# Graph attention on one core: the softmax numerator placed in the one-hot, the relation factor applied by GpSimd, the sums in two banks

## The reference

```python
z = h @ W.T                                   # 6250 x 128
s_src = z @ w1;  s_dst = z @ w2
e = leaky_relu(s_src[src] + s_dst[dst], negative_slope=0.01)
rel_alpha = rel_emb[etype, 0]                 # 40 relations
m = segment_max(e, dst)
num = exp(e - m[dst])
den = segment_sum(num, dst)
alpha = num / den[dst]
h_agg = segment_sum((rel_alpha * alpha)[:, None] * z[src], dst)
return h_agg + bias_w
```

## Time and profile before

| | us |
|---|---|
| median of 3 executions | 10841.97 (10825.0 to 10871.25) |
| profiled execution, its time | 10860.68 |
| profiled execution, its span | 10859.2 |
| attention stage, first to last `look_all` | 3316.4 to 5276.4 |

### The profile page before, as it was taken

The page is one execution under the profiler, slowest core; times in us unless marked ns, Lnnn a source line. Parts: engine busy times, 40 slices in busy tenths (PEclk is TensorE's granted clock), DMA queues, the critical chain, the costliest instruction groups (busy, mean ns, idle before and its releaser), DMA issues. The chain is left out here.

```text
span 10859.2 us, 155042 instructions
## 1 busy us (share of the span) xinstructions
PE 8132.9 (75%) x38400; PEld 4994.6 (46%) x38401; DVE 4174.1 (38%) x9924; ACT 3269.5 (30%) x5403; POOL 5556.4 (51%) x5296
## 2 busy tenths in 40 slices
PE   2988888888875666655688897986887777777776
PEld 1544444444444555555433333333344555555554
DVE  5877777644335666665400000000002222222223
ACT  3012345655555665555200000000002222222222
POOL 5887887777720000000254556555435656566664
PEclk7999999999995666666788898997897777777777
DMA  3234455666644333222466676775672222222222
GB/s 111 75 112 142 150 186 199 222 209 207 214 172 143 121 114 106 98 91 90 175 238 263 241 287 231 290 282 195 262 270 85 62 58 61 59 62 62 62 60 55
DMA packets 563155, 1661.18 MB, mean 153 GB/s; under 512 B 115313, under 2 KB 312029, under 8 KB 519494
## 3 DMA queue, kind: packets, MB, share of 16 engines
q1 hardware_dynamic: 324442, 1129.76, 28.1%
q0 software_dynamic: 206976, 473.99, 14.9%
q10 hardware_dynamic: 31536, 54.94, 1.4%
HBM read 1174.46 MB, written 483.82 MB: 153 GB/s over the span
## 5 line engine op out<-in xcount | busy, mean ns | idle before, releaser
L920 PE MATMUL wide<-ring 128*128 128x392 bf16 x14112 | 2524.8, 340 | 551.8 <-DVE ring L850 269.1
L527 POOL DMA_INDIRECT z_got<-z_table,z_idx x1568 | 2102.0, 1341 | 595.2 <-issue 467.3
L1701 POOL DMA_INDIRECT l_rows<-h_table,l_recs x1568 | 1581.2, 1008 | 1169.9 <-DMA l_recs<-sorted_recs 720.7
L920 PEld LDWEIGHTS wide<-ring 128*128 128x128 bf16 x14112 | 1413.1, 100 | 1663.3 <-issue 907.3
L1610 POOL DMA_INDIRECT sorted_recs<-dn_rec_in,type_f x1568 | 1527.0, 974 | 1251.3 <-DMA dn_rec_in<-in_records 787.1
L1415 PE MATMUL wide<-stream,X 128*128 128x512 f32 (+1 forms) x2548 | 1148.9, 604 | 221.3 <-issue 201.9
L1055 POOL DMA_DIRECT2D rows<-z_edges x196 | 103.5, 528 | 2071.1 <-PE wide L362 1848.4
L373 PE MATMUL wide<-rows,onehot 128*128 128x130 f32 x3904 | 874.9, 413 | 286.2 <-DVE A L390 286.2
L373 PE MATMUL wide<-l_rows,l_onehot 128*128 128x128 f32 x3904 | 657.9, 321 | 503.4 <-issue 299.4
L373 PEld LDWEIGHTS wide<-rows,onehot 128*128 128x128 f32 x3904 | 810.5, 316 | 344.5 <-DVE A L390 344.5
L1415 PEld LDWEIGHTS wide<-stream,X 128*128 128x128 f32 x2548 | 497.5, 203 | 846.1 <-issue 827.5
(11 more groups left out here) (262 smaller groups left out, 8630.4 us busy)
## 6 DMA issues: line engine op xcount, KB each, us to landing
stream<-w_dense SPq DMA_DIRECT2D x252, 1792.0 KB
stream<-c_dense SPq DMA_DIRECT2D x84, 1792.0 KB
z_edges<-z_got POOLq DMA_DIRECT2D x196, 528.0 KB
rows<-z_edges POOLq DMA_DIRECT2D x196, 528.0 KB
dst_bc<-in_dst_row SPq DMA_DIRECT2D x196, 512.0 KB
c_dense<-A SPq DMA_DIRECT2D x49, 1568.0 KB
w_dense<-A SPq DMA_DIRECT2D x49, 1568.0 KB
c_dense<-H SPq DMA_DIRECT2D x49, 1568.0 KB
```

Of the source, the lines that this page charges most:

```text
L527: e.indirect_dma_start(out=z_got[:, s, t, :], out_offset=None, in_=z_table, in_offset=bass.IndirectOffsetOnAxis(ap=z_idx[:, s, t:t + 1], a ...
L920: ins = e.matmul(banks[:, bass.ds(to[v], 1), int(m > 0), 0:WC].rearrange("p a x -> p (a x)"), lhsT=slots[:, k, m * P:(m + 1) * P], rhs=slo ...
L1701: e.indirect_dma_start(out=rows[:, k, t, :], out_offset=None, in_=h_table, in_offset=bass.IndirectOffsetOnAxis(ap=recs[:, k, t, R_DST:R_DS ...
```

## The change

What it does, part by part:

- The one-hot of a tile is now made by `tensor_scalar` with two per-partition scalars: (iota == dst) * num. Eight instructions of 128 elements a pair take the place of two of 512. `num` is not copied into `rows` any more; the column of ones there gives the denominator.
- ACT's eight row scalings are gone. POOL multiplies the rows by the relation factor `rel`, in one `tensor_tensor` of 8 x 128 elements a group, after the DMA has landed.
- The degree is counted by ACT: the mask instruction accumulates into `seen`, a small one adds it to `deg_n`. `add_sums` has one instruction instead of two, and matmuls are 129 instead of 130 columns wide.
- The sums alternate between two banks (`pair_sums`). `half_ready[0]` no longer waits for the addition. The spread source scores alternate too (`s_rowed`), as do the mask (`mask_t`) and `q`. `away` and `mask_t` lie in `H`, which is free in this stage. Addresses that alternate come from a register (`parity`), with a register instruction each.
- ACT makes the masks of group g+1 while DVE is at group g. DVE does the sums of g-1 between the looks of g and `look_all` of g. TensorE turns the scores of g+1 before its looks of g.
- POOL loads three groups at the start; the load of g+3 follows the sums of g-1, and the product for g+1 stands behind it in POOL's queue.
- `s_max` is dropped: `u_node` keeps the running maximum.

```diff
 @block.gpsimd
+                for s in range(SLOTS - 1):
+                    load_rows(slice(s, s + 1), s)
                 with e.Fori(0, TURNS) as i:
                     for s in range(SLOTS):
-                        e.wait_ge(s_free[s], i + 1)
+                        e.wait_ge(s_rows[s], (i + 1) * 16)
                         e.sem_inc(note["pool"], 1)
-                        e.dma_start(rows[:, s, :, :], z_edges[bass.ds(i * SLOTS + s, 1), :, :, :].rearrange(
-                            "a p t w -> (a p) t w")).then_inc(s_rows[s], 16)
+                        e.tensor_tensor(rows[:, s, :, 0:F], rows[:, s, :, 0:F],
+                                        rel[:, bass.ds((i * SLOTS + s) * TILES, TILES)].unsqueeze(2).to_broadcast(
+                                            [P, TILES, F]), ALU.mult).then_inc(s_scaled, 1)
+                        if s == 0:
+                            e.wait_ge(s_free[SLOTS - 1], i + 1)
+                            load_rows(bass.ds(i * SLOTS + (SLOTS - 1), 1), SLOTS - 1)
+                        else:
+                            with e.If(i < TURNS - 1):
+                                e.wait_ge(s_free[s - 1], i + 2)
...
 @block.scalar
-                def scale_rows(g, s):
-                    e.wait_ge(s_w_, g + 1)
-                    for t in range(TILES):
-                        ins = e.activation(rows[:, s, t, 0:F], rows[:, s, t, 0:F], ACT.Copy,
-                                           scale=row_scale[:, t:t + 1])
-                    ins.then_inc(s_scaled, 1)
+                def masks(s, turn):
...
+                    with e.Fori(lo, hi) as b:
+                        at = parity(e, side, c)
+                        e.wait_ge(s_away_free, c)
+                        e.wait_ge(s_look, c)
+                        e.activation(away, dst_bc[:, k, :], ACT.Square, scale=FAR,
+                                     bias=far_node[:, bass.ds(b, 1)]).then_inc(s_away, 1)
+                        e.wait_ge(s_away, c)
+                        e.activation(flat(mask_t[:, bass.ds(at, 1), :]), away, ACT.Relu,
+                                     scale=-1.0, bias=one_f[:, 0:1], accum_out=seen[:, bass.ds(at, 1)]).then_inc(s_ot, 1)
+                        e.wait_ge(s_ot, c)
+                        e.activation(deg_n[:, bass.ds(b, 1)], seen[:, bass.ds(at, 1)], ACT.Identity,
+                                     bias=deg_n[:, bass.ds(b, 1)])
...
+                def ahead(g, s, turn):
+                    pick(s, turn)
+                    bring(g)
+                    masks(s, turn)
...
 @block.tensor
+                        turn_s(g + 1)
+                        looks(g, *ranges[s])
+                        spread_s(g + 1, (s + 1) % 2)
...
                 def sums(g, s, lo, hi):
                     e.wait_ge(s_scaled, g + 1)
-                    pe_sums(e, lo, hi, half_ready, half_done, rows[:, s, :, :], SW_, c2)
-                    mark(e, s_free[s])
+                    with e.Fori(lo, hi):
+                        e.reg_add(c2, c2, 1)
+                        at = parity(e, side, c2)
+                        for h in range(2):
+                            e.wait_ge(half_ready[h], c2)
+                            for t in range(4 * h, 4 * h + 4):
+                                ins = e.matmul(flat(pair_sums[:, bass.ds(at, 1), 0:MW]), lhsT=onehot[:, t, :],
+                                               rhs=rows[:, s, t, 0:MW], start=(t == 0), stop=(t == TILES - 1))
+                            ins.then_inc(half_done[h], 1)
...
 @block.vector
+                def sums(g, s, lo, hi):
+                    e.wait_ge(s_num, g + 1)
+                    with e.Fori(lo, hi) as b:
+                        for h in range(2):
+                            e.wait_ge(half_done[h], c2)
+                            if h:
+                                add_pair(...)
+                            for t in range(4 * h, 4 * h + 4):
+                                ins = e.tensor_scalar(onehot[:, t, :], iota[:, bass.ds(b * P, P)],
+                                                      dst_f[:, bass.ds(g * TILES + t, 1)], num[:, t:t + 1],
+                                                      ALU.is_equal, ALU.mult)
+                            ins.then_inc(half_ready[h], 1)
...
+                        sums(g - 1, s - 1, *ranges[s - 1])
                         e.wait_ge(s_looked, g + 1)
                         e.tensor_reduce(look_all ...)
...
                         e.tensor_tensor(e_edge[:, :], e_edge[:, :], look_all[:, :, 1], ALU.subtract).then_inc(s_ee, 1)
-                        sums(g - 1, s - 1, *ranges[s - 1])
-                        e.wait_ge(s_num, g + 1)
-                        e.tensor_copy(rows[:, s, :, F], num[:, :])
-                        e.tensor_tensor(row_scale[:, :], num[:, :], rel[:, bass.ds(g * TILES, TILES)], ALU.mult
-                                        ).then_inc(s_w_, 1)
```

More of the change, by code:

```diff
@@ L25 @@
 ZW = F + 4
[L26 removed]
+S_DST, S_SRC, S_PARTS = F, F + 1, 2 * (F + 2)
 PARTS = 4
@@ L381, in half_onehot, with add_sums @@
                                    ids.to_broadcast([P, 4, P]), ALU.is_equal)
[L383 removed]
+        def add_sums(e, b, width):
             to, new = A[:, bass.ds(b * width, width)], sums_bank[:, 0:width]
[L386 to L390 removed]
             return e.tensor_tensor(to, to, new, ALU.add)
@@ L424, in dve_sums_end @@
             e.sem_inc(note["dve"], 1)
-            add_sums(e, before, width, None if scales is None else scales.before())
+            add_sums(e, before, width)
             e.drain()
@@ L1065, in _, with pick @@
             def _(e):
-                def bring(g, i, s):
-                    e.wait_ge(s_rows[s], (i + 1) * 16)
+                c = counter(e, "l0_act_pairs", 1)
+                side = e.alloc_register("l0_act_side")
+                regs = [range_registers(e, f"l0_act{s}") for s in range(SLOTS)]
+                after = e.alloc_register("l0_act_after")
+                def pick(s, turn):
+                    e.wait_ge(s_rows[s], (turn + 1) * 16)
                     e.sem_inc(note["act"], 1)
@@ L1084, in _ @@
-                c = counter(e, "l0_act_pairs", 1)
-                regs = [range_registers(e, f"l0_act{s}") for s in range(SLOTS)]
+                    e.copy(s_src_t[:, :], turned).then_inc(s_brought, 1)
+                def ahead(g, s, turn):
+                    pick(s, turn)
+                    bring(g)
+                    masks(s, turn)
                 load_range(e, table_dst, 0, regs[0])
-                before, after = e.alloc_register("l0_act_before"), e.alloc_register("l0_act_after")
+                load_range(e, table_dst, 1, regs[1])
@@ L1088, in _ @@
                 for k in range(2):
                     e.sem_inc(s_bcf[k], 1)
-                e.reg_mov(before, 0)
-                for first in (s_away, s_ot, s_q, s_look, s_away_free, s_away_free):
-                    e.sem_inc(first, 1)
-                bring(0, 0, 0)
+                e.sem_inc(s_away, 1)
+                e.sem_inc(s_ot, 1)
+                e.sem_inc(s_sbc, 1)
+                e.sem_inc(s_away_free, 2)
+                e.sem_inc(s_look, 3)
+                e.copy(deg_n[:, :], zero_f[:, 0:1].to_broadcast([P, NB]))
@@ L1095, in _ @@
+                e.drain()
+                ahead(0, 0, 0)
                 with e.Fori(0, TURNS) as i:
@@ L1153, in spread_s, with looks @@
                     for t in range(TILES):
-                        ins = e.matmul(wide[:, t * P:(t + 1) * P],
+                        ins = e.matmul(s_rowed[k][:, t * P:(t + 1) * P],
                                        lhsT=spread[:, t * P:(t + 1) * P], rhs=s_src_t[:, :], start=True, stop=True)
                     ins.then_inc(s_sbc, 1)
+                def looks(g, lo, hi):
+                    e.wait_ge(s_ee, g + 1)
+                    e.sem_inc(note["pe"], 1)
+                    e.matmul(look, lhsT=zero_h[0:1, :], rhs=zero_h[0:1, 0:6 * TILES], start=True, stop=False)
+                    with e.Fori(lo, hi):
+                        e.reg_add(c, c, 1)
+                        at = parity(e, side, c)
+                        e.wait_ge(s_ot, c)
+                        e.wait_ge(s_q, c)
+                        e.sem_inc(note["pe"], 1)
+                        for t in range(TILES):
+                            ins = e.matmul(look[:, 6 * t:6 * t + 6],
+                                           lhsT=flat(mask_t[:, bass.ds(at, 1), t * P:(t + 1) * P]),
+                                           rhs=flat(q[:, bass.ds(at, 1), :]), start=False, stop=False)
+                        ins.then_inc(s_look, 1)
+                    e.matmul(look[:, 0:1], lhsT=zero_h[0:1, :], rhs=zero_h[0:1, 0:1], start=False, stop=True
+                             ).then_inc(s_looked, 1)
                 def sums(g, s, lo, hi):
@@ L1259, in _ @@
                             e.tensor_copy(m_node[:, bass.ds(b, 1)], m_now[:, 0:1])
-                            e.reg_add(c_last, c_last, 1)
```

(6 more changed lines are left out.)

236 lines of the change are left out of this document (119 added, 117 removed).

## The result

The changed kernel takes 11,280 us (median of 4 runs, 11,259.6 to 11,314.5) against 10,857 for the kernel before on the same chip: ratio 1.038, 95% interval 1.035 to 1.041. The profiled execution took 11,314 us (span 11,313).

The account below looks back on a forecast made before the run. No engine was full; VectorE's chain was taken to set the attention stage's pace. 10,861 - 77 (VectorE's own sum) + 339 (stall) = 11,123, or 11,104 beside the median, said as 11,100 us; range 11,000 to 11,290, 8 in 10: 10,750 to 11,290.

Parts of the forecast that it names:

- The new instruction on GpSimd: Attention stage: GpSimd's product, taken as 2.45 us, locks out VectorE instructions meanwhile, +339 us; chance 0.55.
- a stall of 1.9 a group from phases: VectorE beside the product: middle of 1.3 (only the one-hot waits) to 2.4 (the chain waits at once), for 148 groups.
- Rounds with two looks, for which I had 1.2: 48 two-block groups: stall of 1.2 us each, as part of the product falls beside the second hid, which isn't hindered.
- The cases named in advance: VectorE beside GpSimd's product: two SBUF inputs and tensor_scalar wait; hid and the addition, with an input in PSUM, go on.
- One-block rounds: Attention groups with one block, undisturbed by GpSimd: VectorE alone sets the pace, 7.63 us against 7.29, +67 us over 196 groups.
- Two-block groups: 48 attention groups: second sums 3.9 us after the first, not 5.41; second hid 3.35 after, not 4.86; 1.5 saved each.
- Together 48 x 3.0 = -144 us: 48 two-block attention groups: savings of 1.5 us on the second sums and 1.5 on the second hid.
- the 5.41 that I took for the step before: Two-block groups of the kernel before: the second pair of sums begins 5.41 us after the first, TensorE idling 1.58.
- where I had 3.35: Second look of two-block groups: VectorE's own chain, 2.94 + 0.4, decides when the second hid follows the first.
- the +248 beside the skill's rule: Attention stage: total change stated if VectorE and GpSimd fully block each other by the skill's rule; without it -77.
- VectorE's own sum: Attention stage without GpSimd's disturbance: +67 us for one-block rounds and -144 for two-block groups, -77 us.

Follow-up runs that it names:

- x1: Changed kernel without GpSimd's product, the relation factor left out of the sums; ratio 1.0026 to the kernel before.
- g: Kernel before with one part of the change alone, the two alternating banks of sums; ratio 0.9878 to the kernel before.
- x8: x1 with two wide one-hots of 512 columns a block in place of eight tensor_scalar with the numerator; ratio 0.9915 to the kernel before.
- x7: Changed kernel with GpSimd's product held until e_edge of its own group is finished, so beside hid; ratio 1.0083 to the kernel before.
- x9: x7 with the looks' mask chosen by a branch and not by register addresses; ratio 1.0101 to the kernel before.
- x6: Changed kernel with one wait before GpSimd's product, met a group early, so that it moved nothing; ratio 1.0380 to the kernel before.
- h: g with two mask buffers added, chosen by a register in each address; ratio 0.9986 to the kernel before.
- x4: Changed kernel with the relation factor put on the rows by ScalarE, eight activations a group, GpSimd only loading; ratio 1.0127 to the kernel before.

## Why the forecast was right, and where it was off

**The new instruction on GpSimd: right in its mechanism, and in its size partly by luck.** The product takes 1.91 and not 2.45. I had a stall of 1.9 a group from phases and 339 us in all; 1.87 and 365 were measured, by the stretched instructions and by leaving the product out (364). The stall didn't shrink with the product because the product catches the chain at once, in `q` or `m_step`, and not half-way, so that it costs its full length. I had a product 0.54 too long that met the chain too late, and the two errors offset each other. Rounds with two looks, for which I had 1.2, weren't much cheaper: 14.20 - 12.52 = 1.68, against 1.85 in one-block rounds. The lock holds in the direction that the trace of before did not show. The cases named in advance behaved so: two SBUF inputs and `tensor_scalar` wait, `hid` doesn't. The addition lay beside no product in any run, so of it nothing is shown. To these comes one that I had not named, the copy into `q` (47 of the 193). The Trainium skill (GPSIMD Engine Reference, section "Elementwise — side-by-side cycle accounting") gave an estimate of 2.25 for the product; the trace has 1.91, and decides.

**One-block rounds: right.** In the round above, the steps are 0.76, 0.67, 5.01, 0.87, 1.03, 0.26 and 1.03, sum 9.63; I had 0.77, 0.40, 2.94, 0.55, 1.20, 0.35 and 1.42, 7.63, and a stall. Less the 1.98 by which L1322 exceeds its 0.16 it is 7.65. The steps behind `e_edge` and in front of the one-hot were too short by 0.3 each, those of the one-hots too long by as much: four tiles take 1.03 from first start to the addition's. Against before it is +0.44 (x1: 8.02 to 7.58), for which I said 0.34.

**Two-block groups: wrong.** This is the step that failed: "Together 48 x 3.0 = -144 us". From the table, a second sum cost 12.69 - 7.58 = 5.11 before and 12.50 - 8.02 = 4.48 in x1; a second look 4.99 and 4.50. Saved 0.63 + 0.49 = 1.1 and not 3.0: 54 us. With 195 x 0.44 = 86 us for all rounds the sum is +32, and x1 shows +35, where I had -77. What I left out, as far as runs show it: in g the second sum costs 4.28, so the bank itself gives 0.8. The longer one-hots are not why it isn't more: x8, with wide ones, has 11.95 - 7.13 = 4.82. TensorE and its hand-overs to VectorE set this step, as the rows around a second block's sums show (x7):

```profile
4211.43 0.35 DVE L1266 SCALAR_TENSOR_TENSOR A<-A,m_scale,wide  x1
4211.69 1.11 DVE L1283 TENSOR_SCALAR onehot<-iota,dst_f,num 128x128 f32 x4
4211.81 4.37 PE L1203 MATMUL wide<-rows,onehot 128*128 128x129 f32 x20 [0.30 <-DVE onehot L1283]
4214.05 1.12 DVE L1283 TENSOR_SCALAR onehot<-iota,dst_f,num 128x128 f32 x4 [1.24 <-PE wide L1203]
4216.00 0.35 DVE L1266 SCALAR_TENSOR_TENSOR A<-A,m_scale,wide  x1 [0.83 <-PE wide L1203]
```

From addition to addition it is 4.57, not 3.9. TensorE starts the first block 0.38 after the first addition, as soon as it has a half of the one-hot. Its 16 records of that block last 3.65, to 4215.46, and the second addition starts 0.54 after that. I had the 16 records and a short hand-over, and took them for the whole step. VectorE waits for TensorE twice in it, 1.24 and 0.83. Besides, the 5.41 that I took for the step before is one row, and the mean is 5.11.

In a second look the masks did come earlier, and `hid` follows `hid` after 3.9, where I had 3.35 (x1, 4021.07 and 4024.96). But then TensorE is late: two looks of 1.1 each, with addresses from registers, behind a transposition (L1162) that waits for ScalarE's pick, and that behind both masks. Rows of x1:

```profile
4021.07 1.28 DVE L1299 CUSTOM_DVE_ANT_0 hid<-wide,H,small 128x1024 f32<-128x1024 f32 x1 [1.62 <-issue]
...
4024.96 1.28 DVE L1299 CUSTOM_DVE_ANT_0 hid<-wide,H,small 128x1024 f32<-128x1024 f32 x1 [0.66 <-issue]
...
4027.22 0.22 ACT L1077 COPY s_src_p<-rows 128x32 bf16<-128x32 bf16 x1 [0.20 <-issue]
...
4027.59 0.27 PE L1162 MATMUL wide<-ident_h,s_src_p 128*32 128x128 bf16 x1 [5.87 <-ACT s_src_p L1077]
...
4030.66 1.08 PE L1183 MATMUL wide<-q,H 128*128 x8 [0.88 <-issue]
...
4032.15 0.21 DVE L1333 TENSOR_REDUCE look_all<-wide 128x16 f32<-128x48 f32 x1 [0.58 <-PE wide L1187]
```

The branch saved 0.4 of such a round in x9. What the order in TensorE's queue costs (the transposition in front of the looks) wasn't tried, so the rest of the second look's cost is read from these rows and not shown by a run.

**Together.** 10,861 - 77 + 339 was forecast, that is +262 (the +248 beside the skill's rule does not follow from these terms), and +35 + 364 = +399 is what the stage shows. Of the 137 between them 112 are VectorE's own sum. This miss is larger than what the range allowed for that sum (-25 to +47). The time lies in the range because the range was wide enough for the stall, which is luck. The paired medians differ by 423. The rest isn't the change's: on one chip the time outside the stage was 7599 us in x1, 7596 in x6 and 7610 in g, which is the kernel before outside the stage's sums.

## What to carry to other kernels

Before work goes to GpSimd, list what VectorE runs beside it: here a GpSimd instruction that reads SBUF cost VectorE its full length where a copy of three columns, a `tensor_scalar` or anything with two SBUF inputs was next, however small, and beside `hid`, with an input in PSUM, only what stuck out behind it. One wait in front of it made most of the difference (1.038 to 1.008). Test the parts of a change one by one: here the two banks alone gain 1.2%, and the other parts ate it. When a buffer is doubled, see what chooses the buffer: an address from a register in each of eight short matmuls cost more than the buffer brought back, and a branch around fixed addresses did not.

## What the runs showed of the hardware

- A GpSimd memset, which reads nothing, leaves two-input instructions alone (170 lay within one, none stretched), but stretches `tensor_scalar` on 128x128 float32 and a copy of three bf16 columns to its end; a copy of one float32 column was not (99 lay within one).
- The wait doesn't end with one GpSimd instruction. Near the end of the changed kernel's stage three products follow each other without a load between them, and a copy of three columns, 0.17 by its median, was held through all three:

```profile
5639.05 5.82 DVE L1306 COPY q<-s_dst_p  x1
5639.23 5.60 POOL L1049 TENSOR_TENSOR rows<-rows,rel 128x1024 f32<-128x1024 f32 x3
```
- Eight matmuls of 6 columns with weights at a register's address took 1.06 us by the median in h (0.81 to 1.19) against 0.35 with fixed addresses in g. In h a register operation stands on the queue of the weight loads for each (min/median/max ns):

```profile
L1204 PEldq FUSED_REGOPS  x1952: 46/46/57, 3317.2 to 5264.6; - x196
```

- ScalarE rewrote `rows` while VectorE worked, and neither got longer (x4: 1568 activations of 0.386 by the median, as in the kernel before; 311 one-hot tiles and 70 of VectorE's reads of `rows` began beside them, none stretched).
